# Retention, FP4 feed-forward and two layer norms on one core: scores in 32x32 tiles, attention rows in two PSUM banks, fewer identity products, a new order

## The reference

```python
q, k = rope(x @ Wq), rope(x @ Wk)              # 8 heads of 16
v, g = x @ Wv, x @ Wg                          # 8 heads of 32
scores = einsum('bhqd,bhkd,hqk->bhqk', q * 16**-0.5, k, decay)   # causal, decay**(q-k) by head
o = einsum('bhqk,bhkd->bhqd', scores, v)
o = o * rsqrt(mean(o*o, -1) + 1e-5) * g_norm_w
x = layernorm(x + (o * silu(g)) @ Wo)
h = silu(fp4(x) @ fp4(w_gate).T) * (fp4(x) @ fp4(w_up).T)        # 352 wide
x = layernorm(x + fp4(h) @ fp4(w_down).T)
```

## Time and profile before

| | before |
|---|---|
| median of 3 runs | 134.37 us |
| the profiled execution: its time, its span | 134.68 us, 132.9 us |
| PE busy | 121.9 us, 92% |
| DVE busy | 109.8 us, 83% |
| ACT busy, POOL busy | 88.7 us, 87.8 us |

### The profile page before, as it was taken

One profiled execution on the slowest core, in us unless ns is written; L12 is line 12 of the kernel. 1 busy time (PEld: TensorE's weight loads), 2 busy tenths in 40 slices (PEclk: granted clock), 3 DMA queues, 4 the chain that ended last, 5 costly groups with the idle time before them and its releaser, 6 DMA issues.

```text
span 132.9 us, 5148 instructions
## 1 busy us (share of the span) xinstructions
PE 121.9 (92%) x2072; PEld 86.5 (65%) x2072; DVE 109.8 (83%) x329; ACT 88.7 (67%) x311; POOL 87.8 (66%) x124
## 2 busy tenths in 40 slices
PE   4898789999999999999999999899999899999860
PEld 4764447675676576766666577557686688887650
DVE  1239796789689999999999999799999999999810
ACT  3143465573865849576676759687777787899883
POOL 5012443548859667894956688486949797996781
PEclk9999999999999999999999999999999999999999
DMA  3799991000000000000000000000000000010222
GB/s 91 246 282 358 427 435 69 0 7 7 0 5 0 5 5 0 5 2 5 0 7 0 0 5 2 5 5 0 0 5 5 1 21 0 14 50 20 62 79 79
DMA packets 4791, 7.68 MB, mean 58 GB/s; under 512 B 800, under 2 KB 3872, under 8 KB 4512
## 3 DMA queue, kind: packets, MB, share of 16 engines
q1 hardware_dynamic: 3744, 6.60, 14.2%
q10 hardware_dynamic: 1024, 0.76, 1.8%
HBM read 6.31 MB, written 1.05 MB: 55 GB/s over the span
## 4 chain that ended last, share of the span: by engine, by line
PE 73%; DVE 12%; ACT 4%; issue 4%; DMA 3%; POOL 2%; POOLq 0%; DVEq 0%; ACTq 0%
PE ps L313 9%; PE ps L441 7%; PE ps L307 6%; PE ps L421 6%; PE ps L427 6%; PE ps L330 5%; PE ps L355 4%; PE ps L365 4%; PE ps L341 3%; PE ps L301 3%; PE ps L433 3%; PE ps L386 3%; DMA w_qk<-in_w_qk 3%; DVE probs L728 3%; PE ps L387 2%
## 5 line engine op out<-in xcount | busy, mean ns | idle before, releaser
L860 POOL TENSOR_TENSOR rstd_h<-ms,minus_half 128x8 f32<-128x8 f32 x16 | 26.8, 1674 | 7.6 <-DVE ms L744 7.5
L855 POOL TENSOR_TENSOR qk<-rope 128x256 f32<-128x256 f32 x16 | 11.7, 731 | 11.2 <-DVE rope L722 11.2
L313 PE MATMUL ps<-w_vg,xT_sb 128*128 128x512 f32 x32 | 16.7, 604 | 0.5 <-DVE S L739 0.5
L879 POOL TENSOR_TENSOR xq<-x_ratio,xs 128x128 f32<-128x128 f32 x16 | 7.9, 491 | 11.5 <-DVE x_ratio L657 11.5
L722 DVE TENSOR_TENSOR rope<-ps,tabs_sb 128x512 f32<-128x512 f32 x16 | 11.0, 686 | 5.4 <-PE ps L307 5.2
L441 PE MATMUL ps<-wd_T,hT 128*128 128x128 f32 x96 | 14.1, 283 | 1.3 <-DVE r L758 0.7
L871 POOL TENSOR_TENSOR rstd<-veps,minus_half 128x1 f32<-128x1 f32 x16 | 9.3, 581 | 7.7 <-DVE veps L753 7.7
L887 POOL TENSOR_TENSOR hq<-h_ratio,hs 128x352 f32<-128x352 f32 x16 | 13.1, 816 | 1.7 <-DVE h_ratio L657 1.3
L441 PEld LDWEIGHTS ps<-wd_T,hT 128*128 128x128 f32 x96 | 12.1, 191 | 3.1 <-ACT hT L484 1.5
L421 PE MATMUL ps<-wgu_T,xqT 128*128 128x352 f32 x32 | 13.3, 496 | 0.0
L728 DVE TENSOR_TENSOR probs<-ps,causal 128x512 f32<-128x512 f32 x16 | 11.0, 690 | 2.4 <-PE ps L330 2.0
(11 more groups left out here) (110 smaller groups left out, 349.0 us busy)
## 6 DMA issues: line engine op xcount, KB each, us to landing
tabs_sb<-rope_tables SPq DMA_DIRECT2D x1, 2048.0 KB, 12.4
tabs_sb<-rope_tables SPq DMA_DIRECT2D x1, 1280.0 KB, 8.3
out<-x SPq DMA_DIRECT2D x16, 64.0 KB, 1.5
tabs_sb<-rope_tables SPq DMA_DIRECT2D x1, 512.0 KB, 4.3
xT_sb<-x_transposed SPq DMA_DIRECT2D x1, 512.0 KB, 7.9
xT_sb<-x_transposed SPq DMA_DIRECT2D x1, 320.0 KB, 5.6
tabs_sb<-rope_tables SPq DMA_DIRECT2D x1, 256.0 KB, 4.0
w_vg<-in_w_vg ACTq DMA_DIRECT2D x1, 256.0 KB, 4.4
```

Source lines behind the costliest of these rows:

```text
L313: mm(vg_ps, xT(c), w_vg[:], start=True, stop=True).then_inc(vg_pe, 1)
L855: gp.tensor_tensor(g16(qk[:, c % D, :]), g16(rope[:, c % D, 0, :]), g16(rope[:, c % D, 1, :])[:, :, ::-1, :], ALU.add).then_inc(qk_p, 1)
L860: gp.tensor_tensor(rstd_h[:, c, :], ms[:, c, :], minus_half[:], ALU.pow).then_inc(rms_p, 1)
```

## The change

1. `scores`: 16 products on 32x32 tiles in place of 8 on 32x64.
2. `oT` takes banks 1 and 2 in place of 0 to 3. A bank holds one half a; in it the even heads are in columns 0 to 63 and the odd heads in 64 to 127, and pair j in partitions 32j to 32j + 31. So head n is written by array column group j = n // 2, where before it was n % 4. Two sums share a bank's quadrant, so only the first product (e = 0) carries the start flag. ACT and DVE (`copy_oT`, `squares`, `gated`) read the new layout by other access patterns of the same size.
3. Other tenants move: `qkT` to bank 3, `o` to 2, `xqT` to 1, `hT` to 0, and the weight transposes to banks 1 and 0. `qkT` and `hT` no longer share a bank with `oT`.
4. SP issues the load of x for chunks 1 and 2 before it waits for the first rope table, not behind that wait.
5. The three `warm_up(4)` behind `transpose_qk` of chunks 0, 1 and 2 go. The two before it stay.
6. PE, ACT, DVE and POOL get new lists, and `h_ratio_` waits for POOL's reader of the buffer that it overwrites.

```diff
-        BANKS = {"sc": (0, 1, 2, 3), "oT": (0, 1, 2, 3), "o": (1,), "yT": (7,), "qk": (4,), "qkT": (0,),
-                 "vg": (6,), "att": (5,), "xqT": (2,), "gate": (4,), "hT": (3,), "up": (7,),
+        BANKS = {"sc": (0, 1, 2, 3), "oT": (1, 2), "o": (2,), "yT": (7,), "qk": (4,), "qkT": (3,),
+                 "vg": (6,), "att": (5,), "xqT": (1,), "gate": (4,), "hT": (0,), "up": (7,),
...
-        oT_ps = ps[:, 0:4, 0:CH]
-        oT_bank = lambda half, a: ps[:, BANKS["oT"][2 * half + a], 0:CH]
+        oT_ps = ps[:, 1:3, 0:C].rearrange("p a (e q) -> p a e q", q=CH)
+        oT_bank = lambda a, e: ps[:, BANKS["oT"][a], CH * e:CH * e + CH]
...
             load_tables(0)
+            load_x(1)
             sp.wait_ge(d_tab[0], 16)
-            load_x(1)
...
-                for a in range(2):
+                for k in range(4):
                     for j in range(NP):
...
-                        last = mm(sc_ps(j)[CH * a:CH * a + CH, :], kT[rows, c % D, CH * a:CH * a + CH],
-                                  q_eo[rows, c % D, a, :, :].rearrange("p e q -> p (e q)"), start=True, stop=True)
+                        rows, keys = slice(32 * j, 32 * j + 32), slice(32 * k, 32 * k + 32)
+                        last = mm(sc_ps(j)[keys, :], kT[rows, c % D, keys],
+                                  q_eo[rows, c % D, k // 2, :, :].rearrange("p e q -> p (e q)"), start=True, stop=True)
...
                 for a in range(2):
                     for n in range(NH):
-                        j, e, slot32 = n // 2, n % 2, n % 4
+                        j, e = n // 2, n % 2
                         rows = slice(32 * j, 32 * j + 32)
-                        mm(oT_bank(n // 4, a)[32 * slot32:32 * slot32 + 32, :],
-                           S[rows, (2 * c + a) % 8, e * DV:(e + 1) * DV], q_eo[rows, c % D, a, e, :], start=True, stop=False)
+                        mm(oT_bank(a, e)[rows, :], S[rows, (2 * c + a) % 8, e * DV:(e + 1) * DV],
+                           q_eo[rows, c % D, a, e, :], start=e == 0, stop=False)
...
                 for n in range(NH):
-                    slot32 = n % 4
+                    j, e = n // 2, n % 2
                     for a in range(2):
...
-                        last = mm(oT_bank(n // 4, a)[32 * slot32:32 * slot32 + 32, :],
-                                  v_sb[keys, c % D, n * DV:(n + 1) * DV], probs[keys, c % D, n, :], start=False, stop=True)
+                        last = mm(oT_bank(a, e)[32 * j:32 * j + 32, :],
+                                  v_sb[keys, c % D, n * DV:(n + 1) * DV], probs[keys, c % D, n, :], start=False, stop=e == 1)
...
-            warm_up(4); project_qk(0); warm_up(4); project_vg(0); transpose_qk(0); warm_up(4); project_qk(1)
+            warm_up(4); project_qk(0); warm_up(4); project_vg(0); transpose_qk(0); project_qk(1); state_product(0)
...
+                if c >= 6:
+                    dve.wait_ge(hq_p, c - 5)
```

More of the change, by code:

```diff
@@ L449, in _ @@
-            out_projection(0); transpose_y(1); project_qk(4); from_state(2); state_product(3); values(2)
-            project_qk(5); transpose_o(2); transpose_qk(3); out_projection(1); state_product(4); scores(3)
-            project_qk(6); from_state(3); values(3); project_qk(7); transpose_qk(4); transpose_o(3); transpose_y(2)
-            transpose_xq(0); project_vg(5); gate(0); scores(4); out_projection(2); from_state(4); state_product(5)
-            values(4); project_qk(8); transpose_o(4); transpose_qk(5); transpose_y(3); project_vg(6); transpose_xq(1)
@@ L464, in _ @@
-            values(10); project_qk(14); transpose_o(10); transpose_qk(11); project_vg(12); transpose_xq(7)
-            transpose_y(9); scores(11); up(6); out_projection(9); from_state(11); state_product(12); values(11)
-            gate(7); transpose_qk(12); transpose_o(11); transpose_y(10); project_vg(13); project_qk(15); up(7)
-            transpose_xq(8); out_projection(10); scores(12); gate(8); from_state(12); values(12); state_product(13)
-            transpose_o(12); transpose_qk(13); transpose_y(11); project_vg(14); transpose_xq(9); up(8); scores(13)
@@ new lines, in _ @@
+            transpose_down_weights(); scores(2); project_vg(4); out_projection(0); transpose_y(1); project_qk(4)
+            from_state(2); state_product(3); values(2); project_qk(5); transpose_o(2); transpose_qk(3)
+            out_projection(1); project_qk(6); scores(3); state_product(4); from_state(3); values(3); transpose_qk(4)
+            project_qk(7); transpose_o(3); transpose_y(2); transpose_xq(0); project_vg(5); gate(0); scores(4)
+            out_projection(2); from_state(4); state_product(5); values(4); transpose_qk(5); project_qk(8)
@@ new lines, in _ @@
+            transpose_o(4); transpose_y(3); project_vg(6); transpose_xq(1); up(0); scores(5); out_projection(3)
+            from_state(5); state_product(6); values(5); gate(1); transpose_o(5); transpose_qk(6); transpose_y(4)
+            project_vg(7); project_qk(9); transpose_xq(2); up(1); scores(6); out_projection(4); from_state(6)
+            state_product(7); values(6); gate(2); transpose_o(6); transpose_qk(7); transpose_y(5); project_vg(8)
+            project_qk(10); transpose_xq(3); up(2); scores(7); out_projection(5); from_state(7); state_product(8)
@@ new lines, in _ @@
+            values(7); transpose_qk(8); gate(3); transpose_o(7); transpose_y(6); project_vg(9); project_qk(11)
+            transpose_xq(4); up(3); scores(8); out_projection(6); from_state(8); state_product(9); values(8); gate(4)
+            transpose_qk(9); transpose_o(8); transpose_y(7); project_vg(10); project_qk(12); transpose_xq(5); up(4)
+            scores(9); out_projection(7); from_state(9); state_product(10); values(9); transpose_qk(10); gate(5)
+            transpose_o(9); transpose_y(8); project_vg(11); project_qk(13); up(5); transpose_xq(6); out_projection(8)
@@ new lines, in _ @@
+            scores(10); gate(6); from_state(10); state_product(11); values(10); project_qk(14); transpose_qk(11)
+            transpose_o(10); project_vg(12); transpose_xq(7); transpose_y(9); scores(11); up(6); out_projection(9)
+            from_state(11); state_product(12); values(11); gate(7); transpose_qk(12); transpose_o(11); transpose_y(10)
+            project_vg(13); project_qk(15); up(7); transpose_xq(8); out_projection(10); scores(12); gate(8)
+            state_product(13); from_state(12); values(12); transpose_qk(13); transpose_y(11); transpose_o(12)
@@ new lines, in _ @@
+            project_vg(14); transpose_xq(9); up(8); scores(13); gate(9); out_projection(11); from_state(13)
+            state_product(14); values(13); transpose_h(0); transpose_qk(14); transpose_o(13); transpose_y(12)
+            project_vg(15); up(9); transpose_xq(10); out_projection(12); scores(14); gate(10); from_state(14)
+            state_product(15); values(14); transpose_qk(15); transpose_y(13); down(0); transpose_o(14); transpose_h(1)
+            up(10); out_projection(13); transpose_xq(11); down(1); gate(11); scores(15); up(11); from_state(15)
@@ L628, in _ @@
[L628 to L630 removed]
+            silu_g_(0); copy_v(0); q_odd(0); q_even(0); k_transposed(0); copy_v(1); silu_g_(1); copy_oT(0)
+            weights_magic(0); squares(0); k_transposed(1); q_even(1); q_odd(1); silu_g_(2); copy_v(2); silu_g_(3)
```

225 lines of the change are left out of this document (105 added, 120 removed).

## The result

The changed kernel took 137.47 us (median of 4 runs, 136.94 to 139.22) against 134.47 us for the kernel before on the same chip (4 runs, 134.25 to 134.88): ratio 1.021, 95% interval [1.016, 1.025]. That ratio leaves out the one execution of 139.22 us, which lies 1.7% above the fastest of the four. A second measurement of the same kernel gave 138.04 us (136.68 to 138.52) against 134.38, ratio 1.025 [1.019, 1.031]. The prediction was 134.7 us, between 131.6 and 138.5, with slower as the likeliest of the three outcomes.

The account below looks back on a forecast made before the run. PE was taken to bound the middle, with an unbroken chain of 5.81 us a chunk. 134.68 - 1.4 + 2.0 + 0.3 - 0.6 = 134.98 on the profiled execution, so 134.7 us as median; range 131.6 to 138.5.

Parts of the forecast that it names:

- from_state, +0.2 a chunk: from_state on four tiles instead of eight: step about 0.65 us, charged to 10 of 16 chunks, +2.0 us.
- values, 0: values keeps eight tiles with two products each, only in another sequence: no added time.
- scores, +0.3: scores as 16 products on sixteen tiles: +0.03 us in 10 chunks, +0.3 us, between -0.5 and +3.
- The start, -1.4: Removing three identity groups at the start, early x load included: -1.4 us, between 0 and -2.67.
- Bank moves and order, -0.6: PE's weight loads wait less for copies and q after bank moves and reordering: -0.6 us, between 0 and -3.1.
- Rival 1: Products queue behind a busy tile in from_state and values: 147 us, or about 140 in milder form; chance 0.20.
- Rival 2: DVE bounds the middle as much, so PE's addition vanishes in waits: 132.9 us, between 131.5 and 134; chance 0.32.
- Rival 3: The start gives nothing because DVE's weight work only moves: 136.1 us; chance inside the forecast's 0.48.
- L355 at 0.65: Sign: from_state takes 0.65 us from first start to the next step's if tiles are independent, 1.3 if not.
- L330 at 0.44: Sign: the scores step, 0.41 us on the chain before, takes 0.44 us up to L386.
- the wait of L319: Sign: transpose_qk no longer waits for the copy of oT, a wait of 0.8 us between 30 and 100 us.
- scores(2) at 22.5: Sign at the start: scores of chunk 2 begins at about 22.5 us in place of 23.93.

Follow-up runs that it names:

- the turns experiment: The changed kernel with the heads of from_state and values issued in the order 0 2 4 6 1 3 5 7: 135.93 us, ratio 1.012.
- the rows-only kernel: The kernel before, its order and 64-wide scores kept, with only the attention rows in two banks and the new bank table: 138.74 us, ratio 1.031.
- the shifted kernel: The kernel before with scores in 32x32 tiles and 28 tiny unused identity products (112 records) behind the first identity group: 139.35 us, ratio 1.037.

## Why the prediction was right in direction and short in size

The loss was forecast as 0.3 us and is 3.0 (137.47 - 134.47), or 3.7 by the second measurement. The time lies inside the stated 131.6 to 138.5, but outside the 133.4 to 136.6 that the terms of the sum allowed. The wide range was stretched for the rivals and for a clock lost through the missing groups, not for the terms that failed, so that it held is in part luck; so is the direction, to which 0.49 had been given. The largest term was right in kind; what was missing came from several small ones.

- **from_state, +0.2 a chunk: the size was right, the count wrong.** Measured +0.23 from first to last product, 0.65 to 0.69 us on the chain and 0.62 from its first product to the next step's. The reckoning from streaming time, four products on each of four tiles, held, and the turns experiment shows that the tiles' load is the bound. But I charged 10 of 16 chunks, 2.0 us, and took DVE to cover the rest. The 13 chunks of the middle alone pay 2.6 us, and in the rows-only kernel, with 0.7 for values, all of it shows.
- **values, 0: a term that failed.** The sentence "only in another sequence: 0" was wrong by up to 0.08 us a chunk, 1.0 us in 13. The sequence half 0, half 1, half 0, half 1 keeps the same number of products on a tile and still costs; with another sequence of heads it went to zero.
- **scores, +0.3: the size of the step was right, what came with it was not seen.** Unstalled it costs 0.03 us as estimated. The 32 more records a chunk moved the places where blocks of instructions meet, and cost 0.13 to 0.23 us in each of four chunks of the changed kernel's first profile, 0.8 us together (0.6 in three chunks of the second). And the path from scores over the mask to from_state was taken to have room, where from_state now starts 0.4 to 0.6 us later in all. Against the run with 64-wide scores the middle is 1.3 us longer. That is inside the bounds of -0.5 to +3, but for another reason than the one given for them. In the old order the same edit cost 5.4 us.
- **The start, -1.4: right as a value of the part alone.** The three kernels that differ from before by the groups alone, or by them with the early load or the tiny products, were 1.3 to 1.6 us faster. In the changed kernel's two profiles scores(2) is only 0.3 and 0.75 us earlier. In them PE ran the first products at half rate until 9.8 us and 8.0 us (6.5 before), as the chain of the first shows:

```profile
4.76 1.22 PE ps L307 x2
5.99 1.71 PE ps L301 x8
7.69 1.71 PE ps L313 x2
```

where the kernel before shows

```profile
4.34 1.22 PE ps L307 x2
5.56 1.40 PE ps L301 x8
6.96 0.86 PE ps L313 x2
```

The eight identity records and two projections take 1.71 and 1.71 us here and 1.40 and 0.86 there, and project_qk(0) begins 0.42 us later: with these 1.6 us, -1.4 became about 0 in this profile. The windows give the granted clock as 1.00 all along, but the trace's record of it begins only at 6.49 us before and at 9.84 us here, at full speed, and these are the moments at which the products' pace doubles. Over the thirteen profiles at normal pace PE's products come to the full rate between 5.0 and 9.9 us. But for its last 0.2 us this slow stretch lies ahead of where the first group was removed (behind transpose_qk(0), at 9.62 us here), so the removal isn't its cause. The seven profiles with the early load of x had it at 5.0 to 9.9 us, the four with the late load and no tiny products at 5.3 to 6.5; with a spread that wide I leave open whether the load has part in it.
- **Bank moves and order, -0.6: not found.** from_state, scores, values and the later starts of from_state make 5.2 us in either profile, and 5.2 and 5.0 were measured. With 64-wide scores the same reckoning leaves 0.1 to 0.3 us for it, so at most 0.3. L319's wait for the rows' copy did go, as said; but it was the order that would have made it large, so the gain is a cost avoided, not one won.
- **Rival 1, tiles not independent: refuted.** from_state took 0.62 to 0.69, not 1.3 us, with two products in a row for the same tile. The rule of the Trainium skill ("TensorE: Matmul & The Clock Gate", "The mechanism") that matmuls start and end strictly in order does not hold here across tiles, as far as starts go: besides the 0.62, a record of values starts ahead of the last three of state_product. Of the ends the trace says nothing, since they are modelled. The sequence is worth 0.04 us in from_state and 0.08 in values, a tenth of what the rival asked.
- **Rival 2, absorbed: refuted.** The period in the middle is 6.3 us. It would have needed DVE to be the bound; DVE's busy share in the middle fell instead.
- **Rival 3, the start gives nothing: nearer to the changed kernel than the forecast, for another reason.** Its scores(2) came 0.3 and 0.75 us earlier, not 1.4; but the groups are worth 1.3 to 1.6 us, and what hid them in the first profile is the slow first 10 us and not DVE's weight work.

By the rows that I had named: L355 at 0.65 held (0.62 from its first start to the next step's), L330 at 0.44 held where no block ended, the wait of L319 went, scores(2) at 22.5 did not hold in either profile of the changed kernel (23.5, 23.1), and the period was 6.3 instead of 6.0. The sum by measured terms: -0.3 + 5.2 - 0.4 = +4.5 for the profiled execution.

The best of the kernels is the one before without the three identity groups: 133.0 us, with or without the other edits that cost it nothing.

## What to carry to other kernels

Count the products on each tile of the array, not the products: a step of small matmuls takes at least as long as its fullest tile streams, and on top of that the order in which tiles are visited is worth some hundredths of a microsecond each time. If a step is on PE's unbroken chain in a few chunks, charge it to all of them unless a row shows the cover. A path beside the chain, like the mask here, can be as long as the chain to within some hundredths of a microsecond: ask what slack it has before a step in front of it grows. And where an edit changes the number of instructions in a tight loop, look in the profile for gaps without a cause at fixed distances in records, because the time that it shows may belong to them.

## What the runs showed of the hardware

- Gaps without a releaser of 0.1 to 2.7 us at PE records 193 + 256 k, in most of the kernels; they moved when 48 or 112 records were put ahead of them. In the five of 0.45 us or more the record starts 1.27 to 1.50 us after the end of the 16 KB instruction transfer that belongs to it; in 206 pairs none starts sooner.
- Behind a gap of 2.7 us on PE the granted clock was 0.50 for 3.4 us (17.86 to 21.27 us of the shifted kernel).
- Products on different 32x32 tiles hardly hold each other up: 16 products on four tiles took 0.47 us from first to last start and on eight tiles 0.24, and the difference, 0.23, is the streaming of the two more products that each tile then has, 2 x 0.108 us. Taking the four tiles in turn saved 0.04 of the 0.47.
